# Graph layers on one core: gather steps of one 128-edge tile in place of two

## The chip, the cores and the metric

The kernel runs on one core of a Trainium2 chip. The metric is the device time of one launch in microseconds (us), the median of three runs. TensorE (PE) multiplies matrices into the PSUM banks, VectorE (DVE) and ScalarE (ACT) work elementwise, GpSimd (POOL) here issues the indirect DMAs that gather rows, SyncE (SP) issues the other DMAs.

## What is computed

Four layers with residual connections over 6250 nodes of width 256 and 206250 directed edges, sorted by destination: a graph convolution, a mixture of 8 experts (top 2), a graph attention with 4 heads, and a mixture of 8 experts with a capacity limit. The two graph layers gather one row for each edge and add it up by destination:

```python
# first graph layer (flow stage)
norm = dinv[src] * dinv[dst]
h = x @ W.T
msgs = norm[:, None] * h[src]
out = jax.ops.segment_sum(msgs, dst, num_segments=n)
...
# second graph layer (gat stage)
e = jax.nn.leaky_relu(al_src[src] + al_dst[dst], NEG_SLOPE)
emax = jax.ops.segment_max(e, dst, num_segments=n)
ee = jnp.exp(e - emax[dst])
denom = jax.ops.segment_sum(ee, dst, num_segments=n)
alpha = ee / (denom[dst] + 1e-16)
msg = h[src] * alpha[:, :, None]
out = jax.ops.segment_sum(msg, dst, num_segments=n)
```

## The kernel before

**Blocks, groups, steps, tiles.** The nodes are 49 blocks of 128. The sorted edges are cut into groups of GROUP = T x 128 edges. A *step* is one visit of a block of destinations to one group: a group that straddles two blocks is visited twice, so there are NG + 48 steps. With T = 2 that is 806 + 48 = 854. A *tile* is 128 edges, so a step has T tiles, and every tile of a step is gathered by its own indirect DMA, twice where a group is visited twice. `rank_of_step` holds for each step where its block's rows start in the accumulator `acc`.

**Start stage** (`start_phase`). It counts and orders blocks, gathers each step's edges (`edges_in`, one indirect DMA for sources and one for destinations per 128 steps), turns them on TensorE so that a tile's 128 edges lie on the partitions (`edge_work`, `turn_edges`, `keep_edges`), makes the masks of the attention's running maximum (`tile_masks`), counts degrees (`count_set`) and writes the first row table. ScalarE normalizes and moves the blocks in the same loop in which it keeps the turned edges, in program order.

**Flow stage** (`flow_phase`). GpSimd gathers rows of 768 bf16 values into a ring of RING = 14 steps (28 tiles). For each step TensorE multiplies a one-hot matrix (edge by destination lane) with the gathered rows, three parts for each tile, into one of two PSUM banks `sum_ps`; VectorE adds the bank to `acc` (`add`, line 899). An addition waits for its sum and for the addition before it; TensorE's sum of a step waits for the addition of two steps before. VectorE makes the one-hots of AHEAD = 7 steps in one instruction (line 892), right behind a load of their 7 start addresses into registers (line 110). The expert layer and the products for the next table run beside it: `piece(s, n, c)` puts small parts of the work on earlier blocks behind each step on VectorE and TensorE, numbered by the step s within a quarter of a lap (70 steps, 4 blocks). Each expert is an `up` and a `down` on TensorE.

**Gat stage** (`gat_steps_phase`). The edges go in windows of W = 16 tiles, that is SPW = 8 steps, 107 windows. GpSimd fills a ring of four windows. In each window VectorE makes one-hots for all 16 tiles (line 1535), scans the running maxima, works out the weights' arguments (`edges`), weighs half of the rows (line 1568; ScalarE the other half, line 1729), multiplies what is in `acc` by a fade for the first step (`fold`) and adds each step's sum to `acc` (`add`, line 1583) from one of three banks `sum_ps`. The order in a window is written out in `slot`: a quarter of the sums stands behind the weighing, one behind `segments`, the last two behind `edges`. `tick` slips in the finishing of complete blocks. ScalarE copies a row of `dst_parts` for each step (`pick_dst`).

**Expert stage** (`expert_phase`). The last layer, on tokens sorted into the experts' slots. Nothing in it has to do with steps.

## Time and profile before

| | us |
|---|---|
| median of 3 runs (lowest to highest) | 5138.23 (5134.06 to 5144.11) |
| the profiled execution, its own time | 5136.53 |
| its span in the profile | 5134.7 |
| busy: PE / DVE / ACT / POOL | 3748.7 / 3239.1 / 2421.9 / 3470.0 |
| start stage | 0 to about 191 |
| flow stage (first gather to last work) | 191 to about 2397 |
| gat stage | 2397 to about 4614 |
| expert stage | 4614 to 5135 |

Busy time is an average over stages with different bounds. A wait is put down to what ended last before the engine could go on; "issue" is idle time for which the profile shows no one that was waited for. Issuing and register instructions don't count as busy. Starts and lengths in a timeline overlap a little where an instruction starts while the one before drains.

### The profile page before, as it was taken

How to read it: one execution, taken by the hardware profiler on the slowest of the kernel's cores; microseconds unless marked ns; L12 is line 12 of the kernel's file. 1: busy time of each engine (PE TensorE's matmuls, PEld its weight loads, DVE VectorE, ACT ScalarE, POOL GpSimd, SP SyncE). 2: the span in 40 equal slices, each digit the busy share in tenths (PEclk: the TensorE clock that was granted, in tenths of full speed). 3: DMA queues.
4: the chain of work that ended last, by engine and by line, in shares of the span. 5: the costliest groups of instructions: out<-in, count | busy, mean ns of one | idle time of the engine just before them, and what ended most of it. 6: DMA issues, size and time to landing. Idle time of an engine off the chain costs nothing. (4 is left out here: it accounts for less than half of the span.)

```text
span 5134.7 us, 76750 instructions
## 1 busy us (share of the span) xinstructions
PE 3748.7 (73%) x19865; PEld 2834.2 (55%) x19865; DVE 3239.1 (63%) x9212; ACT 2421.9 (47%) x7596; POOL 3470.0 (68%) x3620
## 2 busy tenths in 40 slices
PE   6277777777777777775667667676777677668998
PEld 4156666666666666564555555454555555545665
DVE  6655555555555555553777777777777777774454
ACT  5323333333333333333666766666766766661221
POOL 4377777777777777774777777777777777742222
PEclk9589999999999999998777777777777777778999
DMA  4656666665665566663455555555555555534221
GB/s 132 204 162 171 170 170 170 170 170 170 170 171 168 168 170 170 170 170 97 138 148 153 148 149 152 147 150 151 151 144 152 148 152 150 148 107 146 75 78 48
DMA packets 338812, 767.24 MB, mean 149 GB/s; under 512 B 79990, under 2 KB 178392, under 8 KB 338238
## 3 DMA queue, kind: packets, MB, share of 16 engines
q0 software_dynamic: 202704, 594.02, 42.2%
q1 hardware_dynamic: 135662, 168.07, 10.0%
...
## 5 line engine op out<-in xcount | busy, mean ns | idle before, releaser
L826 POOL DMA_INDIRECT flow_rows<-table,edges x1708 | 1624.7, 951 | 608.9 <-issue 498.1
L1430 POOL DMA_INDIRECT gat_steps_rows<-table,edges x1712 | 1646.9, 962 | 557.0 <-issue 485.6
L1862 PE MATMUL gat_steps_sum_ps<-gat_steps_rows,gat_steps_onehot 128*128 128x264 f32 x3424 | 1116.1, 481 | 271.1 <-DVE acc L1583 259.1
L1173 PE MATMUL flow_sum_ps<-flow_rows,flow_onehot 128*128 128x256 bf16 x5124 | 779.0, 294 | 412.4 <-DMA flow_rows<-table,edges 319.8
L1862 PEld LDWEIGHTS gat_steps_sum_ps<-gat_steps_rows,gat_steps_onehot 128*128 128x128 f32 x3424 | 761.9, 234 | 479.9 <-DVE acc L1583 303.6
L1173 PEld LDWEIGHTS flow_sum_ps<-flow_rows,flow_onehot 128*128 128x128 bf16 x5124 | 504.8, 105 | 612.7 <-issue 282.2
L1729 ACT ACTIVATE gat_steps_rows<-gat_steps_rows 128x64 f32<-128x64 f32 x3424 | 828.5, 334 | 0.0
L899 DVE TENSOR_TENSOR acc<-flow_sum_ps,acc 128x256 f32 x854 | 359.8, 421 | 660.1 <-PE flow_sum_ps L1173 640.4
L1583 DVE TENSOR_TENSOR acc<-gat_steps_sum_ps,acc 128x264 f32 x856 | 370.5, 433 | 241.0 <-PE gat_steps_sum_ps L1862 165.8
L1225 PE MATMUL flow_y_ps<-flow_w,flow_hid 128*128 128x256 f32 x1568 | 438.5, 405 | 83.4 <-DVE flow_x_blk L985 44.7
L1215 PE MATMUL flow_hid_ps<-flow_xn_t,flow_w 128*128 128x128 f32 x3136 | 459.8, 295 | 8.7 <-ACT flow_hid L1108 8.7
L1215 PEld LDWEIGHTS flow_hid_ps<-flow_xn_t,flow_w 128*128 128x128 f32 x3136 | 429.6, 210 | 24.4 <-ACT flow_hid L1108 15.3
L1108 ACT ACTIVATE flow_hid<-flow_hid_ps,flow_b 128x128 f32<-128x128 f32 x784 | 239.5, 364 | 392.0 <-PE flow_hid_ps L1215 307.4
L892 DVE TENSOR_TENSOR flow_onehot<-flow_iota_ps,edges 128x1792 bf16<-128x1792 f32 x122 | 246.9, 2024 | 195.9 <-issue 104.7
L1225 PEld LDWEIGHTS flow_y_ps<-flow_w,flow_hid 128*128 128x128 f32 x1568 | 280.3, 199 | 147.1 <-issue 59.9
L1808 PE MATMUL gat_steps_lanes_ps<-ident,gat_steps_score 128*64 128x128 f32 x214 | 73.6, 448 | 363.9 <-ACT gat_steps_score L1706 353.6
L1088 ACT ACTIVATE flow_root<-flow_mv,eps 128x1 f32<-128x1 f32 x147 | 43.3, 294 | 607.8 <-DVE flow_mv L923 594.0
...
L1568 DVE TENSOR_TENSOR gat_steps_rows<-gat_steps_rows,gat_steps_weight_ps 128x1024 f32<-128x1024 f32 x214 | 255.5, 1194 | 0.5 <-issue 0.5
L1535 DVE TENSOR_TENSOR gat_steps_onehot<-gat_steps_iota_ps,edges 128x2048 f32<-128x2048 f32 x107 | 243.0, 2271 | 0.0
L1808 PEld LDWEIGHTS gat_steps_lanes_ps<-ident,gat_steps_score 128*64 128x64 f32 x214 | 30.8, 205 | 382.3 <-ACT gat_steps_score L1706 371.9
L2266 PE MATMUL expert_y_ps<-expert_w,acc 128*128 128x256 f32 (+1 forms) x1024 | 223.2, 380 | 5.9 <-ACT acc L2190 5.9
...
## 6 DMA issues: line engine op xcount, KB each, us to landing
gat_steps_drow<-drow SPq DMA_DIRECT2D x107, 512.0 KB
gat_steps_rows<-table,edges POOLq DMA_INDIRECT x1712
flow_rows<-table,edges POOLq DMA_INDIRECT x1708
...
```

Of the source, the lines that this page charges most:

```text
L826: nc.gpsimd.indirect_dma_start(out=rows[n % RING][:, t, :], out_offset=None, in_=g["table0"][:, :], in_offset=bass.IndirectOffsetOnAxis(ap ...
L892: v.tensor_tensor(onehot[k][:, :, :], iota_ps[:, :].unsqueeze(1).broadcast_to([P, AHEAD * T, P]), dst, ALU.is_equal).then_inc(onehot_ready, 1)
L899: v.tensor_tensor(into, sum_ps[i % 2][:, :], into, ALU.add).then_inc(added, 1)
L1173: ins = t.matmul(sum_ps[i % 2][:, :], onehot[i // AHEAD % 2][:, i % AHEAD * T + u, :], rows[i % RING][:, u, part * D:(part + 1) * D], star ...
L1215: ins = t.matmul(hid_ps[e % 2][:, f, :], w1[:, e, c, f * P:(f + 1) * P], xn_t[k % 2][:, c, :], start=(c == 0), stop=(c == KC - 1))
L1225: ins = t.matmul(y_ps[(e + 1) % 2][:, 0:D], hid[e % 2][:, f, :], w2[:, e, f, :], start=(f == 0), stop=(f == KC - 1))
L1430: nc.gpsimd.indirect_dma_start(out=rows[w % RING][:, t, 0:RW], out_offset=None, in_=g["table1"][:, :], in_offset=bass.IndirectOffsetOnAxis ...
L1535: v.tensor_tensor(onehot[k][:, :, :], iota_ps[:, :].unsqueeze(1).broadcast_to([P, W, P]), dst, ALU.is_equal).then_inc(onehot_ready, 1)
L1568: v.tensor_tensor(msg, msg, weight_ps[:, tiles, :].unsqueeze(3).broadcast_to([P, QT, H, C]), ALU.mult).then_inc(weighed, 1)
L1583: v.tensor_tensor(into, sum_ps[(w * SPW + s) % BANKS][:, :], into, ALU.add).then_inc(added, 1)
L1729: ins = s.activation(msg[:, 0:C], msg[:, 0:C], ACT.Copy, scale=msg[:, C:C + 1])
L1862: ins = t.matmul(sum_ps[(w * SPW + s) % BANKS][:, :], onehot[k][:, i, :], rows[r][:, i, :], start=(i == s * T), stop=(i == s * T + T - 1))
```

## The change

T becomes 1: a group is one tile of 128 edges, and so is a step. There are 1612 groups and 1612 + 48 = 1660 steps; the gat stage has SPW = 16 steps in each window of 16 tiles and 104 windows. What is written per step is now done per tile: the sum in its own bank, the addition to `acc`, the start address and, in gat, the copy of `dst_parts`. The start stage takes its edges in 14 sets of 128 steps (SQ), worked on in pairs (PAIR), so that what is turned keeps its size; its tables along the steps are twice as wide, and some share memory. In flow the ring is 17 tiles, one-hots and start addresses come for 17 steps at a time, a lap is 136 steps, and a piece of the other work stands behind every second step.

```diff
@@ -19,7 +19,7 @@
 NB = -(-NODES // P)
 TAIL = NODES - (NB - 1) * P
 EDGES = 206250
-T = 2
+T = 1
 GROUP = T * P
 NG = -(-EDGES // GROUP)
 NGP = NG + 1
@@ -31,7 +31,8 @@
 SPW = W // T
 NW = -(-STEPS // SPW)
 STEPS4 = NW * SPW
-SQ = -(-STEPS4 // P)
+PAIR = 2
+SQ = -(-STEPS4 // (P * PAIR)) * PAIR
@@ -165,10 +166,10 @@
         SET = 7
         SETS = NB // SET
         EDGES_AT = (1, 3, 5)
-        LAST = NGP - (SQ - 1) * P
-        assert SETS * SET == NB and EDGES % GROUP and 0 < LAST <= P
-
-        iota_f = sb("iota_f", [P, SQ * P])
+        FULL = NGP // P
+        LAST = NGP - FULL * P
+        assert SETS * SET == NB and EDGES % GROUP and 0 < LAST and FULL < SQ == SETS * PAIR
+
...
@@ -250,9 +253,11 @@
         dinv_t_ps = small_ps[0:NB, 330:330 + P]
         dinv_ps = small_ps[:, 460:460 + NB]
         reach_ps = small_ps[:, 32:32 + 2 * NB]
-        edge_ps = ps("edge_ps", T * P).rearrange("p (t e) -> p t e", t=T)
+        edge_ps = ps("edge_ps", PAIR * P).rearrange("p (t e) -> p t e", t=PAIR)
         xt_ps = [ps(f"xt_ps{k}", 512).rearrange("p (c n) -> p c n", c=KC) for k in range(2)]
-        row_ps = [ps(f"row_ps{k}", D) for k in range(2)]
+        row_banks = [ps(f"row_ps{k}", 512) for k in range(2)]
+        row_ps = [bank[:, 0:D] for bank in row_banks]
+        step_ps = [bank[0:1, :] for bank in [ps(f"step_ps{k}", 512) for k in range(2)] + row_banks]
...
@@ -459,23 +462,30 @@
                 ch.link(v.reciprocal(var[:, c], var[:, c]))
                 v.scalar_tensor_tensor(offset[:, c], mean[:, c], -1.0, var[:, c], ALU.mult, ALU.mult).then_inc(scales_ready, 1)
 
-            def edge_work(q):
-                at_least(dve, edges_turned, 3 * (q - 1))
-                ds_, nx_ = dst_s[:, q, 0:GROUP], dst_s[:, q, 1:GROUP + 1]
-                v.tensor_copy(work[q % 2][:, 0, :], src_s[:, q, :])
-                ch.link(v.tensor_scalar(work[q % 2][:, 1, :], ds_, blk[:, q:q + 1], None, ALU.subtract))
-                v.tensor_tensor(work[q % 2][:, 2, :], ds_, nx_, ALU.not_equal).then_inc(work_ready, 1)
-                v.tensor_scalar(drow[:, q, :], work[q % 2][:, 1, :], -1.0, float(P), ALU.max, ALU.min)
+            def edge_work(m):
+                at_least(dve, edges_turned, 3 * (m - 1))
+                both = slice(m * PAIR, (m + 1) * PAIR)
+                ds_, nx_ = dst_s[:, both, 0:GROUP], dst_s[:, both, 1:GROUP + 1]
+                src, dst, last = (work[m % 2][:, n, :].rearrange("p (u e) -> p u e", u=PAIR) for n in range(3))
+                v.tensor_copy(src, src_s[:, both, :])
+                for u in range(PAIR):
+                    q = m * PAIR + u
+                    ins = v.tensor_scalar(dst[:, u, :], dst_s[:, q, 0:GROUP], blk[:, q:q + 1], None, ALU.subtract)
+                ch.link(ins)
+                v.tensor_tensor(last, ds_, nx_, ALU.not_equal).then_inc(work_ready, 1)
+                v.tensor_scalar(drow[:, both, :], dst, -1.0, float(P), ALU.max, ALU.min)
 
...
@@ -500,11 +510,11 @@
             set_scales(0)
             set_scales(1)
             dve.wait_ge(edges_in, 32 * SQ)
-            for q in range(SQ):
+            for q in range(SETS):
                 edge_work(q)
                 if q + 2 < SETS:
                     set_stats(q + 2)
-                if q == SQ - 1:
+                if q == SETS - 1:
                     tile_masks()
                 if q:
...
@@ -552,7 +562,7 @@
             def keep_edges(n):
                 q, arr = divmod(n, 3)
                 act.wait_ge(edges_turned, n + 1)
-                out = g["edges"][arr][:, q * P * T:(q + 1) * P * T].rearrange("e (s t) -> e t s", t=T)
+                out = g["edges"][arr][:, q * PAIR * P:(q + 1) * PAIR * P].rearrange("e (u s) -> e u s", u=PAIR)
                 s.copy(out, edge_ps[:, :, :]).then_inc(edges_kept, 1)
 
...
@@ -650,19 +660,18 @@
                 q, arr = divmod(n, 3)
                 pe.wait_ge(work_ready, q + 1)
                 at_least(pe, edges_kept, n)
-                for tt in range(T):
+                for tt in range(PAIR):
                     ins = t.transpose(edge_ps[:, tt, :], work[q % 2][:, arr, tt * P:(tt + 1) * P], g["ident"][:, :])
                 ins.then_inc(edges_turned, 1)
 
...
@@ -694,10 +703,10 @@
     with ExitStack() as ctx:
         sb, ps, sem = memory(nc, ctx, "flow")
 
-        RING = 14
-        AHEAD = 7
-        LAP = 70
-        STARTS = (0, 18, 35, 53)
+        RING = 17
+        AHEAD = 17
+        LAP = 136
+        STARTS = (0, 34, 68, 102)
         PER = 4
         NA = RW + H
         LAPS = STEPS // LAP
@@ -1053,9 +1062,10 @@
                                 if whole or step + AHEAD < STEPS:
                                     onehots(j * (LAP // AHEAD) + (i // AHEAD + 1), (i // AHEAD + 1) % 2)
                             add(step, i, starts[i % AHEAD])
-                        if isinstance(j, int) and j == 0 and c == 0 and s == 6:
+                        if isinstance(j, int) and j == 0 and c == 0 and s == 12:
                             prepare_weights()
-                        piece(s, n, c)
+                        if s % 2 == 0:
+                            piece(s // 2, n, c)
                 if whole:
@@ -1271,11 +1281,12 @@
                     for s in range(length):
                         if not isinstance(j, int) or j * LAP + at + s < STEPS:
                             sums(j, at + s)
-                        if isinstance(j, int) and j == 0 and c == 0 and s == 8:
+                        if isinstance(j, int) and j == 0 and c == 0 and s == 16:
                             turn_weights()
                         if isinstance(j, int) and j == 0 and c == 2 and s == 0:
                             pe.wait_ge(aug_ready, 1)
-                        piece(s, n, c)
+                        if s % 2 == 0:
+                            piece(s // 2, n, c)
 
```

**Order on VectorE, flow stage,** around the one-hots in the loop (`x_blk` is the block's running sum over experts, `front_ps` holds router logits). Before:

```order
L110 TENSOR_LOAD rank_of_step
L103 REGISTER_ALU
L892 ISA
L892 TENSOR_TENSOR flow_onehot1<-flow_iota_ps,edges1 128x1792
L897 REGISTER_ALU
L899 ISA
L899 TENSOR_TENSOR acc<-flow_sum_ps0,acc 128x256
L981 REGISTER_ALU
L987 SCALAR_TENSOR_TENSOR flow_x_blk0<-flow_y_ps0,flow_comb0,flow_x_blk0 128x256
L897 REGISTER_ALU
L899 ISA
L899 TENSOR_TENSOR acc<-flow_sum_ps1,acc 128x256
```

Now:

```order
L111 TENSOR_LOAD rank_of_step
L901 ISA
L901 TENSOR_TENSOR flow_onehot0<-flow_iota_ps,edges1 128x2176
L906 REGISTER_ALU
L908 ISA
L908 TENSOR_TENSOR acc<-flow_sum_ps1,acc 128x256
L906 REGISTER_ALU
L908 ISA
L908 TENSOR_TENSOR acc<-flow_sum_ps0,acc 128x256
L963 TENSOR_REDUCE flow_s1<-flow_front_ps 128x1
L67 REGISTER_ALU
L964 TENSOR_SCALAR flow_lg<-flow_front_ps,flow_s1 128x8
```

The load and the one-hots are wider and come for 17 steps; two additions, with a wait each (the ISA rows), stand one behind the other where before a piece stood behind each.

**Order on VectorE, gat stage,** from the fade on; before:

```order
L1576 TENSOR_TENSOR acc<-acc,gat_steps_fade1 128x260
L1583 TENSOR_TENSOR acc<-gat_steps_sum_ps0,acc 128x264
L1583 ISA
L1583 TENSOR_TENSOR acc<-gat_steps_sum_ps1,acc 128x264
L1526 SCALAR_TENSOR_TENSOR gat_steps_with_left<-gat_steps_mask0,gat_steps_lanes_ps,gat_steps_run_max 64x128
```

Now:

```order
L1587 TENSOR_TENSOR acc<-acc,gat_steps_fade1 128x260
L1594 TENSOR_TENSOR acc<-gat_steps_sum_ps0,acc 128x264
L1594 ISA
L1594 TENSOR_TENSOR acc<-gat_steps_sum_ps1,acc 128x264
L1594 ISA
L1594 TENSOR_TENSOR acc<-gat_steps_sum_ps2,acc 128x264
L1594 ISA
L1594 TENSOR_TENSOR acc<-gat_steps_sum_ps0,acc 128x264
L1537 SCALAR_TENSOR_TENSOR gat_steps_with_left<-gat_steps_mask0,gat_steps_lanes_ps,gat_steps_run_max 64x128
```

Four additions follow the fade where there were two; the same holds behind `segments`, and behind `edges` eight stand in a row where there were four.

**Order on TensorE, gat stage,** from a window's start (`run_max` ends, then sums, carries, `seg_max`). Before:

```order
L1828 MATMUL gat_steps_lanes_ps<-ident,gat_steps_run_max 128x64 x2
L1862 MATMUL gat_steps_sum_ps2<-gat_steps_rows1,gat_steps_onehot1 128x264 x2
L1862 MATMUL gat_steps_sum_ps0<-gat_steps_rows1,gat_steps_onehot1 128x264 x2
L1836 MATMUL gat_steps_lanes_ps<-ones,gat_steps_carry 64x1 x2
L1862 MATMUL gat_steps_sum_ps1<-gat_steps_rows1,gat_steps_onehot1 128x264 x2
L1862 MATMUL gat_steps_sum_ps2<-gat_steps_rows1,gat_steps_onehot1 128x264 x2
L1844 MATMUL gat_steps_terms_ps<-ident,gat_steps_seg_max 128x64
L1862 MATMUL gat_steps_sum_ps0<-gat_steps_rows1,gat_steps_onehot1 128x264 x2
```

Now:

```order
L1839 MATMUL gat_steps_lanes_ps<-ident,gat_steps_run_max 128x64 x2
L1873 MATMUL gat_steps_sum_ps2<-gat_steps_rows2,gat_steps_onehot0 128x264
L1873 MATMUL gat_steps_sum_ps0<-gat_steps_rows2,gat_steps_onehot0 128x264
L1873 MATMUL gat_steps_sum_ps1<-gat_steps_rows2,gat_steps_onehot0 128x264
L1873 MATMUL gat_steps_sum_ps2<-gat_steps_rows2,gat_steps_onehot0 128x264
L1847 MATMUL gat_steps_lanes_ps<-ones,gat_steps_carry 64x1 x2
L1873 MATMUL gat_steps_sum_ps0<-gat_steps_rows2,gat_steps_onehot0 128x264
L1873 MATMUL gat_steps_sum_ps1<-gat_steps_rows2,gat_steps_onehot0 128x264
L1873 MATMUL gat_steps_sum_ps2<-gat_steps_rows2,gat_steps_onehot0 128x264
```

The matmuls stand in the same places, but each has a bank to itself, so the three banks come round after three tiles and not after six.

## Rows read from the trace of the kernel before

**Rows 1.** Costliest groups, page: busy, mean ns of one | idle before, releaser
```profile
L826 POOL DMA_INDIRECT flow_rows<-table,edges x1708 | 1624.7, 951 | 608.9 <-issue 498.1
L1430 POOL DMA_INDIRECT gat_steps_rows<-table,edges x1712 | 1646.9, 962 | 557.0 <-issue 485.6
```

**Rows 2.** Stretches: length, busy PE, PEld, DVE, ACT, POOL (count), clock, DMA, GB/s
```profile
500.00:2000.00 1500.00, 1157.36 (x7497) 935.56 (x7496) 854.94 (x2281) 511.85 (x1088) 1136.26 (x1195) 0.92 0.60 170
2500.00:4500.00 2000.00, 1404.91 (x6400) 1029.11 (x6401) 1487.12 (x4447) 1364.03 (x5164) 1519.01 (x1580) 0.73 0.53 149
```

**Rows 3.** VectorE's waits in flow, 500 to 2000; then L899's own busy row
```profile
DVE acc L899 <- PE flow_sum_ps L1173: 431.9, 297, 4.4
DVE flow_onehot L892 <- issue: 77.0, 46, 5.8
DVE flow_onehot L892 <- PE flow_sum_ps L1173: 71.0, 39, 5.5
...
500.00:2000.00 1500.00, 251.39 (x597) 0.92 0.60 170
```

**Rows 4.** VectorE's waits in gat, 2500 to 4500: us, times, longest
```profile
DVE gat_steps_pre_max L1496 <- PE gat_steps_lanes_ps L1808: 192.8, 93, 5.9
DVE acc L1583 <- PE gat_steps_sum_ps L1862: 150.4, 270, 1.4
DVE acc L1583 <- DVE acc L1583: 63.6, 309, 0.6
```

**Rows 5.** Timeline, VectorE, flow: start, us, instruction [idle before]
```profile
1498.80 0.48 DVE L987 SCALAR_TENSOR_TENSOR flow_x_blk<-flow_y_ps,flow_comb,flow_x_blk 128x256 f32<-128x256 f32 x1
1500.80 2.02 DVE L892 TENSOR_TENSOR flow_onehot<-flow_iota_ps,edges 128x1792 bf16<-128x1792 f32 x1 [1.52 <-issue]
1502.74 0.41 DVE L899 TENSOR_TENSOR acc<-flow_sum_ps,acc 128x256 f32 x1
1503.35 0.42 DVE L899 TENSOR_TENSOR acc<-flow_sum_ps,acc 128x256 f32 x1 [0.20 <-DVE acc L899]
1503.69 0.15 DVE L959 TENSOR_REDUCE flow_s<-flow_ex 128x1 f32<-128x8 f32 x1
```

**Rows 6.** Timeline, VectorE, gat: two neighbouring additions
```profile
3709.78 0.43 DVE L1583 TENSOR_TENSOR acc<-gat_steps_sum_ps,acc 128x264 f32 x1 [0.20 <-DVE acc L1583]
3710.41 0.43 DVE L1583 TENSOR_TENSOR acc<-gat_steps_sum_ps,acc 128x264 f32 x1 [0.20 <-DVE acc L1583]
```

**Rows 7.** Loads of start addresses (L110): count, ns min/median/max, first and last start
```profile
L110 DVEq TENSOR_LOAD <-rank_of_step x85: 1035/1624/1646, 512.7 to 1989.6; - x85
...
L110 DVEq TENSOR_LOAD <-rank_of_step x98: 593/596/619, 2518.8 to 4483.3; - x98
...
L110 DVEq TENSOR_LOAD <-rank_of_step x1: 1037/1037/1037, 688.6 to 688.6; - x1
...
L110 DVEq TENSOR_LOAD <-rank_of_step x1: 1048/1048/1048, 760.7 to 760.7; - x1
```

**Rows 8.** TensorE's waits, flow 500 to 2000, gat 2500 to 4500
```profile
PE flow_sum_ps L1173 <- DMA flow_rows<-table,edges: 155.2, 162, 3.3
...
PE gat_steps_sum_ps L1862 <- DVE acc L1583: 240.7, 98, 3.6
```

**Rows 9.** Timeline, TensorE, gat: two matmul records are one tile
```profile
3758.93 3.86 PE L1862 MATMUL gat_steps_sum_ps<-gat_steps_rows,gat_steps_onehot 128*128 128x264 f32 x8
...
3766.06 2.94 PE L1862 MATMUL gat_steps_sum_ps<-gat_steps_rows,gat_steps_onehot 128*128 128x264 f32 x12
```

**Rows 10.** Timeline, TensorE, flow: one step's sums, half an expert
```profile
1500.22 0.82 PE L1173 MATMUL flow_sum_ps<-flow_rows,flow_onehot 128*128 128x256 bf16 x6
...
1503.88 1.03 PE L1225 MATMUL flow_y_ps<-flow_w,flow_hid 128*128 128x256 f32 x4
```

**Rows 11.** Timeline, start stage: VectorE's wait for edges, ScalarE's behind it
```profile
42.31 0.29 DVE L465 CAST start_work<-start_src_s 128x256 f32<-128x256 int32 x1 [2.40 <-DMA start_src_s<-in_src,start_grp_i]
...
44.01 0.39 ACT L556 CAST edges<-start_edge_ps 128x256 int32<-128x256 f32 x1 [2.64 <-PE start_edge_ps L654]
```

45 lines of the change are left out of this document (23 added, 22 removed).

## The prediction

> **What bounds the kernel now.** The span is 5134.7 us; the same execution measured 5136.5 us, inside the three timed runs (5134.1 to 5144.1, median 5138.2), so a sum made on the profile holds for the median to about 2 us. A measurement of this kernel can tell about 0.2% (10 us) from no change.
>
> I read the costliest groups first [rows 1]. Two of them hold most of the span: GpSimd issuing one indirect DMA for each tile of 128 edges, 1708 in the flow stage and 1712 in the gat stage, 0.95 us busy each and nearly all idle time behind them put down to "issue", not to another engine. The table of stretches [rows 2] gives their pace: 1195 in 1500 us, or 1.255 us a tile, in flow, and 1580 in 2000 us, or 1.266 us, in gat. 1708 x 1.255 = 2144 us and 1712 x 1.266 = 2167 us: GpSimd sets both stages, 4311 us of 5135.
>
> Next, how far the other engines are behind it. The waits of VectorE in the flow stretch [rows 3]: 431.9 us until TensorE's sums, and 148.0 us ahead of the one-hots. In gat [rows 4]: 192.8 + 150.4 us. TensorE waits 155.2 us for gathered rows in flow, and in gat 240.7 us for banks that VectorE has yet to add [rows 8]. So VectorE has room. How much is the question, since the change is paid on VectorE.
>
> **Need of VectorE, before.** By "need" I mean its time with the waits for other engines taken out. *Gat*: 2000 - 192.8 - 150.4 = 1657 us, less about 10 us of small waits, over 1580/16 = 98.75 windows of 16 tiles: 16.7 us, against GpSimd's 16 x 1.266 = 20.25. *Flow*: of the 148.0 us ahead of the 85 one-hots, about 1.4 us each (1.52 in the row shown [rows 5]) is the load of seven start addresses, 119 us, and 29 us is waiting. Need (1500 - 431.9 - 29)/597 steps = 1.74 us a step; a block has 854/49 = 17.4 steps, so 30.3 us a block, against GpSimd's 34.9 tiles x 1.255 = 43.7.
>
> **The change, part by part.**
>
> *Fewer tiles.* The order of the changed kernel has 1660 and 1664 gathers, 48 fewer in each stage. At the present pace that is -60 us in flow and -61 us in gat. It counts only where GpSimd goes on being the bound: 33.9 tiles x 1.255 = 42.5 us a block, 20.25 us a window.
>
> *Additions.* 854 become 1660 and 856 become 1664. An addition lasts 0.42 to 0.43 us, and each waits for the one before by its own counter. Followed by another instruction it costs 0.34 us from start to start; followed by an addition 0.61 in flow [rows 5] and 0.63 in gat [rows 6], the 0.20 of idle being that wait. Each added addition stands right behind or ahead of another one (pieces come only on even steps; in gat they stand in fours and eights), so I take the full distance: gat 8 x 0.63 = 5.1 us a window, flow 16.5 x 0.61 = 10.0 us a block. The lower bound is the 0.34 (2.7 and 5.6 us).
>
> The Trainium skill ("VectorE: DVE Perf Modes", the section "The DRAIN you can't avoid") says that chaining VectorE operations by semaphores costs nothing over leaving them out. By that, an addition would cost about the 0.34, and this change would be a gain (rival 1). The rows disagree: 0.20 us of idle stands behind an addition whenever another follows, 309 times in the gat stretch [rows 4]; I go by them.
>
> *Start addresses.* Loads on VectorE's queue [rows 7]: 8 values, always at a multiple of four, 0.60 us; 7 values 1.04 us at best and 1.62 us in the median. The short ones come every fourth time (those at 688.6 and 760.7 us have three between them), as 7w is a multiple of four for every fourth w. So it looks like 0.3 us for an aligned four and 0.23 for a single value. Now 16 aligned values a window: 1.2 us, +0.6. In flow 17 values twice a block: once in four 4 x 0.26 + 0.26 = 1.3 us, else 17 x 0.23 = 3.9; mean 3.3, less 0.15 that isn't exposed, so 2 x 3.1 = 6.2 against 2.5 x 1.4 = 3.5: +2.7 us a block. Bounds: 0 (the price is the instruction's) and +4.
>
> *One-hots.* In gat unchanged for a window. In flow 2 of 2176 columns in place of 2.5 of 1792: 2 x 2.45 - 2.5 x 2.02 = -0.1 us. The bytes gathered per tile are the same.
>
> *New need.* Gat 16.7 + 5.1 + 0.6 = 22.4 us a window, above GpSimd's 20.25. Flow 30.3 + 10.0 + 2.7 - 0.1 = 42.9 us a block, level with GpSimd's 42.5. VectorE becomes the bound of gat and ties in flow.
>
> *TensorE's run-ahead.* The banks stay three in gat and two in flow, but each now holds one tile and not two, so TensorE may be 3 (2) tiles ahead of the additions and not 6 (4). In gat VectorE has 4.1 us without an addition (one-hots and edge terms); then eight follow at 0.63, the first three from banks that are full, the other five at the pace of TensorE. A tile costs TensorE 0.96 us in a slow stretch and 0.49 in a fast one [rows 9], granted clock 0.73 in the mean, a mixture of the two levels: at 0.65 it just keeps up, at 0.96 VectorE loses 1 to 2 us a window. VectorE waits 1.5 us a window there now; part of that goes, as the additions are slower to ask. I take 1.0 (bounds 0 and 2.5): 23.4 us. In flow TensorE's steps are uneven. Two tiles' sums (0.82) and one half of an expert (1.03) [rows 10] are 1.9 us, on pieces 7 and 13 to 16 of each block against VectorE's 0.34 + 0.48 + 0.61 = 1.4; piece 8 and piece 10 are wider apart. That is 0.5 to 0.9 us over seven pieces, 4.3 us a block that VectorE can't use, because it can't lag or lead by more than two tiles; elsewhere VectorE is the longer. I take 4.0 (bounds 0 and 8): 46.9 us a block.
>
> *Ring.* In flow it falls from 28 tiles to 17, 21 us of gathers; half a block. That evens out bursts less than before, but a gather started 21 us ahead is not late. Cost nothing; if TensorE falls further back, it is in the 8 above.
>
> *ScalarE in gat.* Eight more copies of 12 columns and a longer load a window, about 1.5 us. It waited for VectorE's results and for rows before, and VectorE's window now grows by more, so nothing is added.
>
> *Start stage.* 28 edge gathers in place of 14, before any destination block is turned: 14 x 1.25 = 17.5 us on GpSimd. Now VectorE waits 2.4 us for the last of them, and ScalarE 2.6 us behind it at 44 us [rows 11], and ScalarE then is the longer engine to the stage's middle, so all of it shows. Tables of twice the width (iota, one-hots, four step slices) add some 5 us, halved count rows give some back. +20 us (10 to 30).
>
> **Sum.** Gat: 104 windows x 23.4 = 2434 against 2167: +267. Flow: 49 x 46.9 = 2298 against 2144: +154. Start +20. Together +441 on 5137: about **5578 us**, 8.6% slower. Expert stage, heads and tails of the stages are kept as they are.
>
> **Rivals.**
> 1. *The additions cost only 0.34, GpSimd stays the bound (faster).* Need in gat 16.7 + 2.7 + 0.6 = 20.0 a window, under 20.25, and in flow 30.3 + 5.6 + 2.7 = 38.6, under 42.5. Then -60 - 61 + 20: 5036 us. It decides at a price of an addition of about 0.37 us in gat. For it: GpSimd's pace is steady now. Against: the 0.20 behind every neighbouring addition, and TensorE still has to come along. 4%.
> 2. *VectorE's bare need.* TensorE always ahead, the long loads cheap: gat 104 x 22.4 = 2330 (+163), flow at 43.5 a block (-12), start +15: 5303, and up to 5400 with one of the two terms present. For it: now that VectorE is late, everything it asks for may be there. 20%.
> 3. *TensorE's clock falls.* The granted clock is 0.92 in flow and 0.73 in gat, where TensorE is idle more often [rows 2]. If more waiting for banks brings it to the lower level (1.2 GHz) most of the time, a tile is 0.96 us in gat: window 24.9 (2590, +423); flow 51 a block (2499, +355), start +25: 5940. From about 5750 on it is this. 14%.
> 4. *Gains and losses cancel*, within 0.2%: needs the first rival in one stage and the forecast in the other. 2%.
>
> **Chances.** The forecast, 5400 to 5750, has 60%. The range from 5310 to 5780 holds it, most of the second rival and a little of the third, about 80%. Faster 0.04, same 0.02, slower 0.94.
>
> **What would show it.** In the profile after: GpSimd's idle time behind its gathers no longer "issue" but until TensorE's sums, and a pace above 1.40 us a tile in gat (23.4/16 = 1.46) and about 1.38 in flow. VectorE busy some 80% in both; no wait for scores of windows (the 192.8 us gone), hardly any idle of TensorE until gathered rows in gat. Loads of start addresses near 1.2 us in gat and 3.9 us in flow in the median. "DVE acc" behind "DVE acc" 0.20 us, above 1000 times. TensorE waiting for VectorE's additions instead of for rows. What would make it wrong: gathers still at 1.26 us in gat, or an addition that costs less behind another.

## The result, and the profile after

The changed kernel takes **5777.2 us** (median of 4, 5772.9 to 5782.9) against 5137.6 in the same comparison: ratio 1.124, interval 1.1226 to 1.1253. It is 640 us slower, where 441 were forecast. The mechanism of the forecast is in the trace; three of its sizes were too small.

The costliest groups, to be held against [rows 1] (busy, mean ns of one | idle before, releaser):

```profile
L835 POOL DMA_INDIRECT flow_rows<-table,edges x1660 | 1578.1, 951 | 943.0 <-PE flow_sum_ps L1183 526.2
L1441 POOL DMA_INDIRECT gat_steps_rows<-table,edges x1664 | 1605.3, 965 | 851.2 <-PE gat_steps_sum_ps L1873 477.2
...
L1183 PE MATMUL flow_sum_ps<-flow_rows,flow_onehot 128*128 128x256 bf16 x4980 | 870.3, 314 | 615.1 <-DVE acc L908 487.5
```

A gather is as long as before (0.951 and 0.965 us), but most of GpSimd's idle time behind them was "issue" and is now until TensorE's sums; and TensorE's own idle time is until VectorE's additions. GpSimd no longer sets either stage. Read backwards, that is a queue: rows are freed by sums, sums by additions.

Each stage by the first and last gather, first the kernel before, then the changed one (durations in ns min/median/max, then first and last start):

```profile
L826 POOL DMA_INDIRECT flow_rows<-table,edges x1708: 942/946/1207, 191.3 to 2335.1; - x190
L1430 POOL DMA_INDIRECT gat_steps_rows<-table,edges x1712: 942/946/1437, 2397.1 to 4564.2; - x191
```

```profile
L835 POOL DMA_INDIRECT flow_rows<-table,edges x1660: 940/946/1198, 227.0 to 2651.2; - x185
L1441 POOL DMA_INDIRECT gat_steps_rows<-table,edges x1664: 940/946/1468, 2733.4 to 5151.5; - x185
```

From these come five stretches: up to flow's first gather, flow's gathers, from its last to gat's first ("gap"), gat's gathers, and the rest. The spans of the profiled executions, 5134.7 and 5771.9, differ by 637.2 = 35.7 + 280.4 + 20.2 + 251.0 + 49.9. The same five for every kernel run here (us; the median beside them is the timed one):

| kernel | median | start | flow | gap | gat | rest |
|---|---|---|---|---|---|---|
| before | 5137.6 | 191.3 | 2143.8 | 62.0 | 2167.1 | 570.5 |
| changed | 5777.2 | 227.0 | 2424.2 | 82.2 | 2418.1 | 620.4 |
| e1, before + second addition, chained | 5380.5 | 193.9 | 2217.8 | 88.7 | 2268.7 | 611.4 |
| e2, the same, unchained | 5163.2 | 191.6 | 2145.4 | 63.3 | 2177.1 | 571.8 |
| e3, changed + loads of eight | 5536.0 | 227.6 | 2160.8 | 75.9 | 2435.6 | 619.5 |
| e4, changed + third bank in flow | 5711.8 | 227.6 | 2326.4 | 80.1 | 2453.1 | 620.6 |
| e5, e3 + iota from SBUF | 5574.5 | 228.6 | 2227.5 | 65.6 | 2420.3 | 617.8 |
| e6, e5 + third bank in flow | 5590.6 | 229.3 | 2241.6 | 63.7 | 2435.1 | 619.7 |
| e7, changed + fourth bank in gat | 5670.5 | 227.9 | 2428.2 | 82.2 | 2320.7 | 616.0 |
| e8, changed + additions in edge terms | 5613.1 | 229.1 | 2426.0 | 82.3 | 2264.5 | 610.9 |
| e9, e3 + e7 + e8 | 5338.2 | 227.3 | 2170.1 | 78.0 | 2247.0 | 610.0 |
| e10, e9 + additions in the chain | 5325.1 | 229.8 | 2171.0 | 78.0 | 2233.5 | 611.4 |
| e11, changed + filled idle in gat | 5765.8 | 230.4 | 2425.1 | 83.9 | 2404.6 | 620.4 |
| e12, changed + one-hots apart | 5964.3 | 226.4 | 2579.4 | 81.2 | 2466.0 | 617.8 |

The stretches of the changed kernel, as in [rows 2] (flow, then all of gat):

```profile
500.00:2000.00 1500.00, 1083.92 (x6458) 847.49 (x6459) 946.78 (x2481) 450.18 (x954) 963.53 (x1015) 0.85 0.52 145
2733.00:5151.00 2418.00, 1668.91 (x6502) 1136.16 (x6502) 1844.63 (x5346) 1463.81 (x6068) 1604.16 (x1663) 0.71 0.46 130
```

1015 gathers in 1500 us are 1.478 us a tile or 50.1 us a block (46.9 forecast); 1663 in 2418 are 1.454 a tile or 23.3 us a window (23.4 forecast). Then VectorE's waits, flow 500 to 2000 and gat 2900 to 4600, with its loads of start addresses in flow between them, to be held against [rows 3, 4, 7]:

```profile
DVE acc L908 <- PE flow_sum_ps L1183: 194.9, 219, 2.9
DVE flow_onehot L901 <- issue: 179.7, 48, 4.6
DVE acc L908 <- DVE acc L908: 88.3, 428, 0.6
DVE flow_onehot L901 <- PE flow_sum_ps L1183: 27.7, 12, 4.7
```

```profile
L111 DVEq TENSOR_LOAD <-rank_of_step x60: 1343/3828/3854, 497.6 to 1979.5; - x60
```

```profile
DVE acc L1594 <- PE gat_steps_sum_ps L1873: 179.3, 518, 0.8
DVE acc L1594 <- DVE acc L1594: 91.5, 446, 0.6
```

The wait for scores, 192.8 us in [rows 4], is gone. The self-wait of an addition, 17 times in flow before, stands there 428 times. The load of 17 addresses lasts 3.83 us, 1.34 where it is aligned, as forecast. And TensorE, same stretches:

```profile
PE flow_sum_ps L1183 <- DVE acc L908: 288.7, 101, 5.5
...
PE gat_steps_sum_ps L1873 <- DVE acc L1594: 343.2, 154, 5.4
```

Its waits for gathered rows, 155.2 us in [rows 8], are gone: the shorter ring costs nothing that shows. Both engines wait for each other in turn, TensorE up to 5.5 us at a time. One such place in gat, VectorE first and then TensorE:

```profile
3500.76 0.43 DVE L1594 TENSOR_TENSOR acc<-gat_steps_sum_ps,acc 128x264 f32 x1 [0.20 <-DVE acc L1594]
...
3502.69 2.26 DVE L1546 TENSOR_TENSOR gat_steps_onehot<-gat_steps_iota_ps,edges 128x2048 f32<-128x2048 f32 x1
...
3506.54 0.43 DVE L1594 TENSOR_TENSOR acc<-gat_steps_sum_ps,acc 128x264 f32 x1
...
3509.26 0.43 DVE L1594 TENSOR_TENSOR acc<-gat_steps_sum_ps,acc 128x264 f32 x1 [0.38 <-PE gat_steps_sum_ps L1873]
```

```profile
3500.35 1.61 PE L1873 MATMUL gat_steps_sum_ps<-gat_steps_rows,gat_steps_onehot 128*128 128x264 f32 x6
3507.03 4.18 PE L1873 MATMUL gat_steps_sum_ps<-gat_steps_rows,gat_steps_onehot 128*128 128x264 f32 x10 [5.07 <-DVE acc L1594]
```

From 3501.2 to 3506.5 VectorE adds nothing (one-hots and edge terms); TensorE fills three banks and stands still for 5.07 us; then the next five tiles take 4.18 us, 0.84 each, more than the 0.63 of an addition, and the additions wait for them.

### The profile page after: what moved, and what is told of

Same layout as the page of the kernel before. It is cut to its first block and busy times, and to the rows that moved or that the text cites. A ratio compares the mean times of both kernels' runs of the same rounds, so it can differ in the third digit from the quotient of the medians.

```text
span 5771.9 us, 83634 instructions
## 1 busy us (share of the span) xinstructions
PE 4082.6 (71%) x19567; PEld 2945.8 (51%) x19567; DVE 3858.4 (67%) x10732; ACT 2475.0 (43%) x8296; POOL 3395.4 (59%) x3538
## 5 line engine op out<-in xcount | busy, mean ns | idle before, releaser
L835 POOL DMA_INDIRECT flow_rows<-table,edges x1660 | 1578.1, 951 | 943.0 <-PE flow_sum_ps L1183 526.2
L1441 POOL DMA_INDIRECT gat_steps_rows<-table,edges x1664 | 1605.3, 965 | 851.2 <-PE gat_steps_sum_ps L1873 477.2
L1873 PE MATMUL gat_steps_sum_ps<-gat_steps_rows,gat_steps_onehot 128*128 128x264 f32 x3328 | 1349.2, 562 | 510.8 <-DVE acc L1594 496.8
L1183 PE MATMUL flow_sum_ps<-flow_rows,flow_onehot 128*128 128x256 bf16 x4980 | 870.3, 314 | 615.1 <-DVE acc L908 487.5
L1873 PEld LDWEIGHTS gat_steps_sum_ps<-gat_steps_rows,gat_steps_onehot 128*128 128x128 f32 x3328 | 844.0, 275 | 873.9 <-DVE acc L1594 670.3
L908 DVE TENSOR_TENSOR acc<-flow_sum_ps,acc 128x256 f32 x1660 | 702.4, 423 | 501.9 <-PE flow_sum_ps L1183 333.1
L1594 DVE TENSOR_TENSOR acc<-gat_steps_sum_ps,acc 128x264 f32 x1664 | 719.8, 433 | 400.4 <-PE gat_steps_sum_ps L1873 260.4
L901 DVE TENSOR_TENSOR flow_onehot<-flow_iota_ps,edges 128x2176 bf16<-128x2176 f32 x98 | 237.5, 2425 | 326.2 <-issue 282.4
L2068 POOL DMA_INDIRECT out<-expert_y,expert_out_id x64 | 64.9, 1015 | 333.8 <-DVE expert_y L2164 328.6
L1724 ACT COPY gat_steps_dst_parts<-dst_parts 128x12 bf16 x1664 | 182.4, 196 | 77.6 <-issue 75.9
L2258 PE MATMUL expert_hid_ps<-expert_xe_t,expert_w 128*128 128x465 f32 (+1 forms) x512 | 214.2, 579 | 1.6 <-ACT expert_xe_t L2193 1.6
```

The costliest lines, as they stand in the source:

```text
L835: nc.gpsimd.indirect_dma_start(out=rows[n % RING][:, t, :], out_offset=None, in_=g["table0"][:, :], in_offset=bass.IndirectOffsetOnAxis(ap ...
L908: v.tensor_tensor(into, sum_ps[i % 2][:, :], into, ALU.add).then_inc(added, 1)
L1183: ins = t.matmul(sum_ps[i % 2][:, :], onehot[i // AHEAD % 2][:, i % AHEAD * T + u, :], rows[i % RING][:, u, part * D:(part + 1) * D], star ...
L1441: nc.gpsimd.indirect_dma_start(out=rows[w % RING][:, t, 0:RW], out_offset=None, in_=g["table1"][:, :], in_offset=bass.IndirectOffsetOnAxis ...
L1594: v.tensor_tensor(into, sum_ps[(w * SPW + s) % BANKS][:, :], into, ALU.add).then_inc(added, 1)
L1873: ins = t.matmul(sum_ps[(w * SPW + s) % BANKS][:, :], onehot[k][:, i, :], rows[r][:, i, :], start=(i == s * T), stop=(i == s * T + T - 1))
```

## Experiments

Theory: VectorE's time is the bound, made of additions at some 0.6 us, long loads in flow, and a coupling by which VectorE and TensorE can't be more than two or three tiles apart. Rivals: TensorE in smaller groups or at a lower clock; only one of the parts.

**The additions alone.** The kernel before, with its tiles of two, its loads and its banks; each step adds its sums a second time:

```
 v.tensor_tensor(into, sum_ps[i % 2][:, :], into, ALU.add).then_inc(first_added, 1)
+dve.wait_ge(first_added, step + 1)
+v.tensor_tensor(extra[:, :], sum_ps[i % 2][:, :], extra[:, :], ALU.add).then_inc(added, 1)
```

> The kernel before (steps of two tiles, 14 steps of ring) in which every step has a second addition of the same sums, into a scratch tile, that waits for the first by a counter, and for which the next step's addition waits in turn: 854 and 856 additions more, nothing else; the output is the same. TensorE's groups, the loads and the tiles are those of before. Theory (each added addition takes 0.61 to 0.63 us of VectorE's time): need in gat 16.7 + 8 x 0.63 = 21.7 us a window against GpSimd's 20.25, so 107 windows of 21.7 to 22.7 us, +155 to +262 us; in flow 30.3 + 17.4 x 0.61 = 40.9 us a block, still under GpSimd's 43.7, so 0 to +50 us. Together 5290 to 5450, I take 5370. Rival (the extra time of the change comes from TensorE working in groups of one tile, or from its clock, not from the additions): under 5180.

In e2 the second one waits for nothing and writes `sum + zero` into one of two scratch tiles.

> As the run before it, but nothing waits for the second addition on VectorE and it waits for nothing there: it adds the sums to a tile of zeros into one of two scratch tiles, and the next real addition waits for the real one alone; the output is the same. Theory (0.20 us of an addition's price is the wait for the one before, and a following instruction covers it): a second addition costs 0.34 us or less, need in gat 16.7 + 8 x 0.34 = 19.4 us a window, under GpSimd's 20.25: 5140 to 5210. Rival (the price is the addition's own work, however it is chained): like the run before, 5290 to 5450.

Measured: e1 5380.5 us (ratio 1.0445, 1.0427 to 1.0462), e2 5163.2 (1.0029, 1.0019 to 1.0039). VectorE does nearly the same work in both. The stretch from 2900 to 4600, e1 and then e2; the third figure is its busy time, 1.14 and 1.10 us for each gathered tile (1448.12/1269 and 1454.33/1319):

```profile
2900.00:4600.00 1700.00, 1236.18 (x5078) 887.85 (x5078) 1448.12 (x4161) 1076.88 (x4102) 1220.27 (x1269) 0.68 0.50 141
```

```profile
2900.00:4600.00 1700.00, 1222.71 (x5400) 888.63 (x5400) 1454.33 (x4433) 1146.31 (x4350) 1276.60 (x1319) 0.73 0.52 147
```

So 1710 additions that wait for nothing on VectorE cost 14 us beside the kernel before, and the same additions in a chain 231 us: the price is the waiting, not the adding. By stretch, e1 is 74 us longer in flow's gathers (0 to 50 expected), 102 in gat's, and 27 and 41 in what follows each. The rival's 5180 is excluded: TensorE's groups of one tile aren't needed to make it slow (whether they add to it in the changed kernel, e1 can't say). In e1's gat, a closer look at three instructions in a row:

```profile
3504.09 0.43 DVE L1590 TENSOR_TENSOR acc<-gat_steps_sum_ps,acc 128x264 f32 x1
3504.56 0.43 DVE L1592 TENSOR_TENSOR gat_steps_extra<-gat_steps_sum_ps,gat_steps_extra 128x264 f32<-128x264 f32 x1
3505.19 0.43 DVE L1590 TENSOR_TENSOR acc<-gat_steps_sum_ps,acc 128x264 f32 x1 [0.20 <-DVE gat_steps_extra L1592]
```

Behind an addition the second one starts after 0.47 us, and behind the second one the next step's after 0.63. These are the medians of all such pairs in e1's gat too (856 and 536 pairs); in e2, where the added one is not waited for, the median behind it is 0.34. Both wait for the instruction just ahead. In the code as compiled they differ: the second addition has one wait and carries it itself, the real one has two (the sums and the addition ahead), and they stand in an instruction of their own ahead of it:

```
L1592 TENSOR_TENSOR gat_steps_extra<-gat_steps_sum_ps,gat_steps_extra 128x264 [waits gat_steps_first_added]
L1590 ISA [waits gat_steps_added,gat_steps_summed]
L1590 TENSOR_TENSOR acc<-gat_steps_sum_ps,acc 128x264
```

So of the 0.29 us by which an addition behind an addition is dearer than elsewhere (0.63 against 0.34), 0.13 comes with one wait on the result just ahead, and 0.16 more with the real addition. That one differs in two things: it has two waits, and its place in `acc` comes from a register; the trace has a FUSED_REGOPS of 46 ns ahead of it in VectorE's queue and none ahead of the second addition. Which of the two costs the 0.16, no run separates. In e2 the real addition has both and starts 0.34 us behind its neighbour, so neither costs anything by itself once the waits are over. e1's second additions, at 0.47, are cheaper than those of the change; an addition with a single wait in the changed kernel wasn't tried.

**The loads of start addresses in flow.**

```
+if i % EIGHT == 0:
+    starts = starts_of(nc, dve, g, step, EIGHT, 0)
 if i % AHEAD == 0:
-    starts = starts_of(nc, dve, g, step, AHEAD, 0)
```

> The changed kernel with the flow stage's start addresses loaded on VectorE as 8 values every 8 steps (always at a multiple of eight) in place of 17 values every 17 steps. Theory (VectorE is the bound in flow, so what it is spared shows in full): 4.25 loads of 0.6 us a block in place of 2 of about 3.1, -3.7 us a block, -180 us, and the stretches in which TensorE fills both banks and stops get shorter: 5777 to between 5560 and 5610. Rival (TensorE at the lower clock bounds flow): -50 us at most, 5725 or more. Gat is the same code and must be the same within 10 us.

Measured 5536.0 us (1.0772, 1.0735 to 1.0808), 241 less than the changed kernel and 24 below the range of the theory. Flow's gathers 263 us shorter, 44.1 us a block against 49.5. The stretch from 500 to 2000, and VectorE's waits in it:

```profile
500.00:2000.00 1500.00, 1154.97 (x7287) 879.38 (x7286) 1064.94 (x2782) 507.18 (x1075) 1095.07 (x1151) 0.93 0.58 164
```

```profile
DVE acc L909 <- PE flow_sum_ps L1185: 201.0, 232, 2.8
DVE acc L909 <- DVE acc L909: 134.9, 500, 0.8
DVE flow_onehot L902 <- PE flow_sum_ps L1185: 31.6, 8, 4.3
```

A block here: (201.0 + 31.6)/33.97 = 6.8 us of waits for TensorE (7.4 in the changed kernel, (194.9 + 27.7)/29.96), 4.0 us of waits behind its own additions (2.9), and no wait on "issue" ahead of the one-hots (6.0). I had charged the 4.25 loads of eight with 0.6 us each, 2.55 us a block; they show as some 1.0 us in the self-waits, the rest is under waits that are there anyway. That is why more came back than the difference of the loads. The clock went from 0.85 to 0.93 with it, but what VectorE waits for TensorE fell by 0.6 us a block, 29 us over the stage, so the clock can't be most of the 263. Gat, with the same code, took 17 us more, where 10 had been allowed.

**Run-ahead in flow.**

```
-sum_ps = [ps(f"sum_ps{k}", D) for k in range(2)]
+sum_ps = [ps(f"sum_ps{k}", D) for k in range(3)]
-at_least(pe, added, step - 1)
+at_least(pe, added, step - 2)
-iota_ps = ps("iota_ps", P)
+iota_ps = g["iota"][:, 0:P]
```

> The changed kernel with three banks for the sums of the flow stage in place of two, so that TensorE may be three tiles ahead (the iota that lay in a bank is read from SBUF instead, and three laps are written out in the loop's body to number the banks). Theory (the 7.3 us a block that VectorE waits for TensorE in flow come from both being held within two tiles of each other): half of it goes, 3 to 4 us a block, 5777 to between 5580 and 5640. Rival (TensorE's own pace is the bound of flow, by its clock): unchanged within 30 us. Second rival (the wait moves to the loads and all is given back): unchanged too, with the idle ahead of the one-hots longer.

Measured 5711.8 us (1.1095, 1.1076 to 1.1113), 65 less: between theory and rival. Flow's gathers are 98 us shorter, 2.0 us a block (3 to 4 expected), and VectorE waits 5.9 us a block for TensorE in place of 7.4; the other 35 us are lost in gat. But the iota's new place had an effect of its own. GpSimd and VectorE, in order of time:

```profile
1504.75 0.95 POOL L837 DMA_INDIRECT flow_rows<-table,edges  x1 [0.30 <-issue]
1505.06 2.43 DVE L903 TENSOR_TENSOR flow_onehot<-iota,edges 128x2176 bf16<-128x2176 f32 x1 [3.68 <-issue]
1506.00 2.30 POOL L837 DMA_INDIRECT flow_rows<-table,edges  x1 [0.30 <-issue]
```

A gather issued while the one-hot instruction runs lasts 2.30 us in place of 0.95: it is done 0.8 us after the one-hots end at 1507.5. In e4 and in e5 98 of flow's 1660 gathers last over 2 us, as many as there are one-hot instructions; in the changed kernel none does. To take this apart, e5 has e3's loads and moves only the iota, e6 adds the third bank.

> The changed kernel with loads of eight in flow (as e3), and the iota of the flow stage's one-hots read from SBUF in place of a bank: two banks for the sums, as in e3. In e4, which reads it so too, a gather issued while a one-hot instruction ran lasted 2.30 us and not 0.95. Theory (VectorE with both operands in SBUF holds up GpSimd's gathers): two gathers a block lose 1.35 us each, and GpSimd's 33.9 x 1.255 = 42.5 us a block become 45.2, above e3's measured 44.2 us a block: +50 us or more on e3's 5536, 5580 to 5640. Rival (e4's long gathers had nothing to do with it, or run-ahead covers them): as e3 within 15 us.

> As e5, with three banks for the sums of flow in place of two (e4's code and loads of eight). Against e5 it shows what run-ahead of one more tile is worth where the long loads are gone. Theory (run-ahead is half of the 4 to 5 us a block that VectorE still waits for TensorE in e3, but GpSimd, at 45.2 us a block by its held gathers, now bounds the stage): 20 to 70 us under e5. Rival (run-ahead is worth nothing once the long loads are gone): e5 within 15 us.

Measured: e5 5574.5 (1.0851), 38 above e3 and a little under the theory's range, because gat and the gap gave 25 us back; flow's gathers are 67 us longer, 45.5 us a block where 45.2 were expected. e6 5590.6 (1.0871) is 16 above e5, where 20 to 70 less were expected; the intervals of the two overlap, so no difference is shown. What TensorE waits for in e6 says why:

```profile
PE flow_sum_ps L1188 <- DMA flow_rows<-table,edges: 198.2, 245, 2.5
PE flow_sum_ps L1188 <- DVE acc L911: 64.7, 81, 1.8
```

It waits for rows again: GpSimd with its held gathers is the bound, and a third bank can't show. So with long loads the third bank and the moved iota together gave 98 us in flow, and the bank by itself was probably worth more, as the iota's move cost 67 in e5; what it would be worth behind short loads with the iota in its bank is open. The Trainium skill ("SBUF — State Buffer", section "SBUF: two separate sides") says that a VectorE instruction with two SBUF inputs and a GpSimd operation that reads SBUF share a pair of ports by an exclusive lock: whichever starts first has it for the whole instruction, and the other is blocked. The 2.30 us agree with it (a gather reads its row numbers from `edges` in SBUF). The other direction doesn't show: the one-hots above start while a gather runs, and take the 2.43 us that they take in the changed kernel with the iota in a bank (2425 ns in the mean).

**Gat: a bank more, and the additions elsewhere.** e7 sets `BANKS = 4`, with the iota in the bank of the weights. e8 hands the second eight additions of a window to the edge terms:

```
 def edges(w, k, r, gap):
     ...
+    gap()            # the next addition that is still owed
     ch.need(n1)      # at each of the seven such waits
```

> The changed kernel with four banks for the sums of gat in place of three (the iota shares a bank with the weights). Theory (gat's 23.5 us a window is VectorE's need plus about 1 us in which it waits for TensorE beyond the 0.2 of its own): one tile more of run-ahead saves 0.3 to 0.9 us a window, 5777 to between 5680 and 5745. Rival (TensorE's pace in its slow stretches bounds gat): unchanged within 15 us.

> The changed kernel with the second eight additions of a gat window placed between the edge terms' instructions (seven places where VectorE waits for its own result) in place of behind them. Same instructions, same loads, three banks. Theory (an addition next to an addition costs 0.63 us and next to another instruction 0.34, and TensorE no longer stands still while eight additions are owed): 7 x 0.3 us of waits less, and the edge terms' own waits covered, 1.2 to 2.4 us a window, 5777 to between 5530 and 5650. Rival (TensorE at the lower clock bounds gat): 5750 or more.

Measured: e7 5670.5 us (1.1027, 1.1009 to 1.1046), 107 less, a little more than the 32 to 97 expected. e8 5613.1 (1.0915, 1.0897 to 1.0933), 164 less, in the theory's range. In e7 the addition again waits for its neighbour in place of for TensorE, from 2900 to 4600 (before the edit 91.5 and 179.3):

```profile
DVE acc L1595 <- DVE acc L1595: 126.4, 621, 0.6
DVE acc L1595 <- PE gat_steps_sum_ps L1874: 90.5, 361, 0.8
```

That is 1.2 us a window of waits for TensorE (90.5/75.9 windows) in place of 2.5 (179.3/72.4). In e8, an addition among the edge terms costs 0.34 us from start to start, and the waits between these are covered:

```profile
3505.62 0.42 DVE L1601 TENSOR_TENSOR acc<-gat_steps_sum_ps,acc 128x264 f32 x1
3505.96 0.26 DVE L1559 TENSOR_TENSOR gat_steps_z<-gat_steps_dst_term,gat_steps_score 128x64 f32<-128x64 f32 x1
```

**TensorE's clock.** In e11, six matmuls that nobody reads fill part of the 5.07 us stop:

```
 def sums(w, k, r, s):
+    if s == 11:
+        for _ in range(6):
+            t.matmul(spare_ps[:, :], onehot[k][:, s, :], rows[r][:, s, :], start=True, stop=True)
```

> The changed kernel with six matmuls of 128x264 into a spare bank in each gat window, that nobody reads, put where TensorE stands still (5.07 us in a window looked at) because its three banks are full and VectorE is at the one-hots and edge terms: 2.9 us of work at the upper level. Otherwise the same. Theory (that stop lowers TensorE's clock, and the eight tiles behind it at 0.8 us each in place of 0.5 keep VectorE waiting): the granted clock in gat rises from 0.72 to 0.80 or more, VectorE's waits for sums shrink, 0.5 to 1.0 us a window, 5777 to between 5670 and 5725. Rival (the clock there isn't due to the stop, or VectorE's need alone sets the window): within 20 us of 5777, or slower by up to 100 where the six matmuls get in the way.

Measured 5765.8 us (1.1215, 1.1196 to 1.1234), 11 less, with an interval that overlaps the changed kernel's: the rival. The granted clock of gat did rise, from 0.71 to 0.76, and the five tiles behind the stop kept up with the additions (below: the six matmuls, those five tiles, and four tiles of the next window):

```profile
2739.00:5144.00 2405.00, 1892.87 (x7704) 1286.32 (x7704) 1848.57 (x5347) 1465.02 (x6072) 1610.78 (x1664) 0.76 0.46 130
```

```profile
3500.15 2.83 PE L1871 MATMUL gat_steps_spare_ps<-gat_steps_rows,gat_steps_onehot 128*128 128x264 f32 x12
3504.03 3.25 PE L1878 MATMUL gat_steps_sum_ps<-gat_steps_rows,gat_steps_onehot 128*128 128x264 f32 x10 [1.04 <-DVE acc L1596]
...
3518.49 3.89 PE L1878 MATMUL gat_steps_sum_ps<-gat_steps_rows,gat_steps_onehot 128*128 128x264 f32 x8
```

Five tiles in 3.25 us are 0.65 each, level with the additions. But four tiles from 3518.49 take 3.89, or 0.97: the slow stretch stands in the window's other half now. In the changed kernel the group at that place took 3.08 us (at 3522.03). VectorE's waits for sums, from 2900 to 4600, are 179.9 us where they were 179.3. Lifting the clock in one place gained nothing; what it would do if it were high in the whole window, e11 doesn't show. e9, below, bears on that: its gat is 171 us shorter than the changed kernel's at a granted clock of 0.70 (2475 to 4722), so a low clock doesn't keep gat slow by itself.

**All of it together.**

> The changed kernel with three of the edits together: loads of eight in flow (e3), four banks in gat (e7), the second eight additions of a gat window between the edge terms (e8). From first to last gather e3's flow was 263 us shorter than the changed kernel's, e7's gat 97 and e8's gat 154. Theory (flow and gat are separate sums, and in gat the bank and the placing cure the same stop of TensorE, so most of e7's gain is in e8's): 5777 - 263 + 24 (what e3 gave back outside flow) - 164 - (0 to 60) = 5315 to 5375, I take 5345. Rival (the two gat edits are independent and add up): 5265 to 5290. Either way slower than the kernel before.

> As e9, with the first eight additions of a gat window spread too: the fold goes ahead of the chain of open maxima, three additions stand in the chain's waits, two between the weighing and the segments. Theory (an addition costs 0.63 us beside another and about 0.34 elsewhere, also here): some five waits of 0.2 to 0.3 less and the chain's own covered, 0.5 to 1.0 us a window, 40 to 100 us under e9. Rival (the first sums of a window aren't there when the chain asks for them, so VectorE waits for TensorE in place of for itself): e9 within 15 us, or slower.

Measured: e9 5338.2 us (1.0387, 1.0369 to 1.0404), in the theory's range. With e8's additions in place, the fourth bank shortens gat by 17 us (2264.5 to 2247.0) and not by 97, so e7 and e8 mostly cure the same stop. e10 5325.1 (1.0361, 1.0343 to 1.0378), 13 less: the rival. VectorE's waits behind its own additions fell from 51.5 to 8.4 us in the stretch from 2900 to 4600, and those for TensorE rose from 72.1 to 106.3. The best version with steps of one tile is 3.6% slower than the kernel before.

**Is it the length of the stop in flow?** Of e3's 5.4 us a block the difference of the loads explains 3.8. In e12 the one-hots stand eight steps behind the long load.

```
-if whole or step + AHEAD < STEPS:
-    onehots(...)
+if i % AHEAD == 8 and (whole or step - 8 + AHEAD < STEPS):
+    onehots(...)
```

> The changed kernel with the flow stage's one-hot instruction eight steps behind the load of 17 start addresses in place of right behind it. Same instructions, same loads, same two banks. Of the 5.9 us a block that e3 took from flow only some 3.8 are the loads' own time (2 of 3.2 us against 4.25 of 0.6). Theory (the rest is TensorE standing still behind two full banks while VectorE adds nothing for 3.8 + 2.4 us in one piece, twice a block): two stops that each find two filled banks in place of one, 0.6 to 2.0 us a block less, 5777 to between 5680 and 5750. Rival (only the load's own time counts, or TensorE's clock, which falls at any stop): within 20 us of 5777.

Measured 5964.3 us (1.1584, 1.1554 to 1.1614), 187 **more**: neither. Flow's gathers are 155 us longer, gat's 48. VectorE's waits, 500 to 2000:

```profile
DVE acc L909 <- PE flow_sum_ps L1184: 325.4, 257, 5.1
DVE acc L909 <- issue: 160.7, 48, 3.8
```

The load's own 5.7 us a block (160.7/28.07) are unchanged, the waits for TensorE rose from 7.4 to 11.6. Eight steps behind the load is a place with a chain that goes through three engines: the one-hots now stand right ahead of the piece that normalizes the token, which TensorE turns and ScalarE copies for the expert matmuls, and ScalarE's and TensorE's own queues are in order. That is at most a part. Counted by place among the 34 additions of a block (per block, additions only, 6.5 to 11.6 us), the waits for TensorE grew by 1.6 us ahead of the 12th and 14th, behind that token; by another 1.6 ahead of the 30th and 32nd, behind the second one-hot instruction, where no token stands; and by 1.5 ahead of the block's first. No run separates the place from the splitting, so the question that e12 was to settle stays open.

## Why the forecast was right, and what it undersized

*Direction and mechanism: right.* VectorE became the bound, by additions that wait for each other, as e1 and e2 show from the kernel before alone (231 us against 14). By the rule of the Trainium skill ("VectorE: DVE Perf Modes", section "The DRAIN you can't avoid") that a semaphore behind each VectorE operation costs nothing extra, e1 and e2 should have taken the same time. The trace doesn't agree: 0.34 us from start to start unchained, 0.47 and 0.63 chained.

*The number: inside the range by 3 us, and that is luck.* 5777.2 lies just under the 5780 of the range, and above the 5750 up to which the forecast had its 60% and from which the prediction would have blamed the clock. That sign was wrong: most of what is above the forecast is in three terms, sized below, and none of them needs the clock.

*Gat: right, with a tail left out.* 23.3 us a window against 23.4. VectorE waits 2.5 us a window for TensorE where 1.0 was assumed, but 0.2 us of each such wait would be the wait for the neighbour anyway, 518 x 0.2/72.4 or 1.4 us, which the forecast had in its price of an addition: 1.1 is left. (8 x 0.63 is 5.0 and not 5.1 us, 10 us over all windows.) But gat's gathers plus what follows them grew by 251.0 + 49.9 us, where 267 were forecast. The 49.9 stand behind the last gather. The expert stage itself is unchanged: its first VectorE instruction is 520.8 us before the span's end (520.3 before). What grew is the way from the last gather to it, 50 to 100 us. When GpSimd is the bound, little lies between its last gather and the last addition, 36.3 us in gat and 4.5 in flow; when VectorE is, the ring is full, and it was 86.8 and 24.1 us, near the rings' content (4 windows x 23.3 = 93, 17 tiles x 1.478 = 25). "Heads and tails of the stages are kept as they are" was the step that failed; it cost 50 us there and 20 in flow's gap.

*Flow: the term "run-ahead" was mis-sized.* 4.0 us a block were assumed, with bounds 0 and 8; VectorE waits 7.4 us for TensorE. Without these, its need is 50.1 - 7.4 = 42.7 us a block, against 42.9 forecast, so additions and loads were right (where an addition waits for TensorE, 0.2 us of it would be its wait for the neighbour anyway: 219 x 0.2/29.96, or 1.5 us a block that could be booked on either side). I had summed only the pieces in which TensorE's work is longer than VectorE's, 7, 8, 10 and 13 to 16. By place among the 34 additions of a block, over half of the additions' waits for TensorE, 106.1 of 194.9 us, stand ahead of the 12th and 14th, behind pieces 5 and 6. There TensorE's own work waits for what VectorE has just made, and the next sum stands behind that work in TensorE's queue. TensorE's waits in the stretch, about once a block each, and then one block, both engines in order of time:

```profile
PE flow_y_ps L1235 <- issue: 34.4, 30, 1.4
PE flow_y_ps L1235 <- DVE flow_x_blk L994: 31.9, 29, 1.2
```

```profile
1446.14 0.42 DVE L1015 TENSOR_TENSOR flow_res<-flow_y_ps,flow_res_bias 128x256 f32<-128x256 f32 x1
1446.66 1.10 PE L1235 MATMUL flow_y_ps<-flow_w,flow_hid 128*128 128x256 f32 x4 [0.71 <-issue]
1448.23 0.42 DVE L908 TENSOR_TENSOR acc<-flow_sum_ps,acc 128x256 f32 x1 [1.66 <-PE flow_sum_ps L1183]
...
1449.66 1.13 PE L1235 MATMUL flow_y_ps<-flow_w,flow_hid 128*128 128x256 f32 x4 [1.24 <-DVE flow_x_blk L994]
1451.47 0.42 DVE L908 TENSOR_TENSOR acc<-flow_sum_ps,acc 128x256 f32 x1 [1.26 <-PE flow_sum_ps L1183]
```

The first expert's `down` waits in the code for the residual (line 1015), the second's for the first y (line 994). Run-ahead helps little there, since both engines are at the same piece: with e4's third bank the two places still take 94.7 us in 31 blocks. Left out as well was that a stop comes back: VectorE adds nothing for 3.8 us of load and 2.4 of one-hots, TensorE fills its two banks and stands still, and its late work is then waited for. That is the 47.0 us ahead of the 22nd addition, the fifth behind a load, 1.6 us a block. Without the long loads (e3) these are 3.2 us, while the two places above stay (133.9 us in 34 blocks). Together: 2424.2 against 2298 us.

*Loads: right as measured* (3.83 us, 1.34 aligned), and the interaction missed: taken away, they give 263 us of flow back and not 181, since short loads hide under other waits.

*Start: +35.7, not +20.* Three rows, GpSimd's and VectorE's:

```profile
31.27 1.12 POOL L318 DMA_INDIRECT start_dst_s<-in_dst_rows,start_grp_i  x1 [28.52 <-DVE start_grp_i L430]
69.47 0.53 DVE L470 CAST start_work<-start_src_s 128x256 f32<-128x256 int32 x1 [21.38 <-DMA start_src_s<-in_src,start_grp_i]
167.88 0.18 DVE L538 TENSOR_TENSOR start_step_flags<-start_span 104x16 f32<-104x16 f32 x1 [7.26 <-DMA start_span<-ends]
```

The first edge gather starts at 31.27 us and not at 22.27, as the wider tables stand ahead of it; the wait for the last one is 21.38 us where it was 2.40 [rows 11]; and a DMA of the spans, hidden before, is waited for 7.26 us. With the 17.5 us of 14 more gathers, which were forecast, that is 9.0 + 17.5 + 7.3 = 33.8 us. I took 5 us for the first and nothing for the last.

*The signs named in advance.* GpSimd's idle time until sums: yes. The wait for scores gone, loads of 3.83 us in flow and 1.10 in gat, 0.20 behind an addition above 1000 times (1337): yes. A pace of 1.46 in gat: yes (1.454). 1.38 in flow: no (1.478). VectorE busy 80%: 76% in gat, 63% in flow; an engine can be the bound and be idle a third of the time, if the waits are its own chain and a partner held close to it.

*The rivals.* That additions cost 0.34: excluded for neighbours. The bare need (5303 to 5400): no, though e9 gets to 5338 by taking the loads away and moving the additions. The clock: it fell to 0.85 in flow and 0.71 in gat. In gat e11 raised it to 0.76 for nothing, and e9 is faster at 0.70; in flow it came back by itself with the short loads, and the waits for TensorE hardly fell. So nothing here shows it setting either stage, though no run holds it high throughout.
